# Graph-attention kernel on one core: segment maxima split into three bf16 terms and looked up in one bf16 product

## The reference

```
def seg_softmax(att, idx, n):
    m = jax.ops.segment_max(att, idx, num_segments=n)
    e = jnp.exp(att - m[idx])
    s = jax.ops.segment_sum(e, idx, num_segments=n)
    return e / (s[idx] + 1e-16)
...
att = seg_softmax(att, col, n)
att_i = seg_softmax(att_i, row, n)
res = (v * att[:, :, None]).reshape(-1, H * DK)
...
agg = jax.ops.segment_sum(res, col, num_segments=n) + jax.ops.segment_sum(res_i, row, num_segments=n)
```

## Time and profile before

| what | value |
|---|---|
| median of 3 runs | 4742.64 us (4734.96 to 4743.93) |
| span of the profiled execution | 4777.7 us |
| first sum stage, first to last `sums` product | about 3000.8 to 3318 us of the span |
| second sum stage, likewise | 4065.1 to 4385 us of the span |
| TensorE busy over the span | 2872.2 us (60%) |
| VectorE busy over the span | 2426.9 us (51%) |

### The profile page before, as it was taken

The page is one execution under the profiler, slowest core; times in us unless marked ns, Lnnn a source line. Parts: engine busy times, 40 slices in busy tenths (PEclk is TensorE's granted clock), DMA queues, the critical chain, the costliest instruction groups (busy, mean ns, idle before and its releaser), DMA issues.

```text
span 4777.7 us, 52094 instructions
## 1 busy us (share of the span) xinstructions
PE 2872.2 (60%) x13590; PEld 1938.9 (41%) x13692; DVE 2426.9 (51%) x4965; ACT 1720.4 (36%) x4345; POOL 2723.8 (57%) x2661
## 2 busy tenths in 40 slices
PE   3200025555533239367677777997777776997588
PEld 1000013333332126223444444887444444886445
DVE  7444444544421001433667677566677777566353
ACT  2232300000011002222455554786555554885451
POOL 5676756666645740466555554788555553555551
PEclk6555557767665569767777777999777777998799
DMA  4343356333414224267766667687777666665300
GB/s 143 113 172 126 143 111 231 89 89 91 98 57 165 97 89 148 68 200 212 216 199 208 200 200 184 177 213 184 205 202 209 201 202 166 160 173 149 110 1 27
DMA packets 767484, 720.00 MB, mean 151 GB/s; under 512 B 389089, under 2 KB 661163, under 8 KB 767068
## 3 DMA queue, kind: packets, MB, share of 16 engines
q1 hardware_dynamic: 645116, 399.08, 29.2%
q0 software_dynamic: 115136, 314.24, 22.4%
q10 hardware_dynamic: 6944, 3.34, 0.2%
HBM read 482.09 MB, written 243.22 MB: 152 GB/s over the span
## 4 chain that ended last, share of the span: by engine, by line
PE 22%; another core or an unknown queue 17%; DVE 16%; issue 12%; ACT 9%; DVEq 4%; POOL 2%; ACTq 2%; DMA 1%; SPq 1%; POOLq 0%
DVE META L1380 5%; DVE BIGR L605 3%; ACT AR L1674 3%; DVE AR L1400 3%; PE ps L1657 2%; PE ps L933 2%; PE ps L944 2%; ACT AR L1676 2%; DVE AR L596 2%; DVEq L1396 2%; PE ps L1480 1%; PE ps L1478 1%; ACTq L1675 1%; PE ps L1428 1%
## 5 line engine op out<-in xcount | busy, mean ns | idle before, releaser
L1349 POOL DMA_INDIRECT AR<-kv_tab,META x832 | 793.7, 954 | 620.8 <-DVE AR L1393 363.1
L1380 DVE TENSOR_REDUCE META<-ps 128x8 f32<-128x1024 f32 x416 | 508.5, 1223 | 186.3 <-remote 94.2
L493 POOL DMA_INDIRECT rec_dst<-AR,slot_e x400 | 403.3, 1008 | 229.1 <-issue 171.0
L625 PE MATMUL ps<-AR 128*128 128x256 f32 x832 | 318.2, 550 | 345.4 <-DVE AR L596 156.4
L579 POOL DMA_INDIRECT AR<-xn_tab,META x416 | 398.6, 958 | 206.8 <-issue 139.0
L1618 POOL TENSOR_TENSOR AR<-AR 128x896 f32<-128x896 f32 x208 | 351.4, 1689 | 246.1 <-ACT AR L1683 241.6
L1583 DVE TENSOR_TENSOR BIGR<-BIGR,ps 128x260 f32 x832 | 354.3, 426 | 217.4 <-PE ps L1657 131.1
L1478 PE MATMUL ps<-AR,identb 128*128 128x512 bf16 x832 | 403.8, 485 | 79.1 <-issue 55.2
L1657 PE MATMUL ps<-AR 128*128 128x260 f32 x1664 | 413.9, 392 | 2.1 <-POOL AR L1618 2.0
L625 PEld LDWEIGHTS ps<-AR 128*128 128x128 f32 x832 | 219.7, 277 | 445.1 <-issue 214.9
L1526 ACT ACTIVATE AR<-ps 12x512 bf16<-12x512 bf16 x208 | 122.1, 587 | 671.8 <-remote 469.9
(11 more groups left out here) (430 smaller groups left out, 5624.0 us busy)
## 6 DMA issues: line engine op xcount, KB each, us to landing
v_dst<-AR SPq DMA_DIRECT2D x104, 384.0 KB
AR<-v_dst SPq DMA_DIRECT2D x104, 384.0 KB
v_src<-AR SPq DMA_DIRECT2D x104, 384.0 KB
AR<-v_src SPq DMA_DIRECT2D x104, 384.0 KB
AR<-in_W_qvk SPq DMA_DIRECT2D x44, 608.0 KB
rec_raw<-AR SPq DMA_DIRECT2D x40, 640.0 KB
AR<-rec_dst SPq DMA_DIRECT2D x104, 192.0 KB
AR<-rec_src SPq DMA_DIRECT2D x104, 192.0 KB
```

Source lines behind the costliest of these rows:

```text
L493: pool.indirect_dma_start(rec_tab[0], bass.IndirectOffsetOnAxis(ap=slot_e[0][:, c * CC + k:c * CC + k + 1].bitcast(U32), axis=0), RD[s][0] ...
L625: ins = pe.matmul(l0_ps(s, u), OW[s][:, u, :], GA[s][:, u, :], start=True, stop=True)
L1349: pool.indirect_dma_start(KVR[s][:, u, 0:KV], None, kv_tab, bass.IndirectOffsetOnAxis(ap=META[o][:, g * U + u, 0:1].bitcast(U32), axis=0)) ...
L1380: ve.tensor_reduce(BMALL[o][:, g * U + 2 * half:g * U + 2 * half + 2, :].rearrange("p b h -> p (b h)"), PSA[:, 2048 + 1024 * half:3072 + 1 ...
```

## The change

The maxima are no longer kept in f32 for the product. After the scans, VectorE splits each f32 maximum into three bf16 terms `M3` (the upper half of the number, the upper half of the rest, and what remains). `lookup` then multiplies the transposed one-hot, now stored in bf16, with the 12 columns of three terms by four heads. `argument` first adds the three terms on VectorE into `MSUM` and then subtracts as before. Buffers move in SBUF to make room.

```
-        OH = [ar(7680 + 512 * s, U, P) for s in range(SL)]
-        OT = [ar(9728 + 512 * s, U, P) for s in range(2)]
+        OH = [ar(8641 + 512 * s, U, P) for s in range(SL)]
+        OT = [ar(a, U, P, dt=BF16) for a in (11201, 5504)]
+        MSUM = [ar(a, U * H1) for a in (7680, 7696)]
...
-        DIST2 = [DIST, ar(11330, U, P)]
+        DIST2 = [ar(a, U, P) for a in (10689, 4992)]
...
-        MT = ar(4160, NB, H1)
+        M3 = AR[:, 4160:4160 + 3 * 3649].bitcast(BF16).rearrange("p (k n) -> p k n", k=3)[:, :, 0:NB * H1].rearrange("p k (b h) -> p k b h", h=H1)
+        MT, MREST = ar(5760, NB, H1), ar(8641, NB, H1)
...
             for h in range(H1):
-                ins = ve.tensor_tensor_scan(MT[:, ::-1, h], EDGE[:, NB:0:-1], BMALL[o][:, ::-1, h], -1.0e30, ALU.add, ALU.max)
-            ins.then_inc(sem("pass_set"), 1)
+                ve.tensor_tensor_scan(MT[:, ::-1, h], EDGE[:, NB:0:-1], BMALL[o][:, ::-1, h], -1.0e30, ALU.add, ALU.max)
+            ve.drain()
+
+            def upper(x):
+                return x.rearrange("p b h -> p (b h)").bitcast(BF16).rearrange("p (b h two) -> p b h two", h=H1, two=2)[:, :, :, 1]
+
+            ve.tensor_copy(M3[:, 0, :, :], upper(MT))
+            ve.tensor_tensor(MREST, MT, upper(MT), ALU.subtract)
+            ve.drain()
+            ve.tensor_copy(M3[:, 1, :, :], upper(MREST))
+            ve.tensor_tensor(M3[:, 2, :, :], MREST, upper(MREST), ALU.subtract).then_inc(sem("pass_set"), 1)
             ve.drain()
...
+                ve.tensor_reduce(MSUM[g % 2], PS[2 + g % 2][:, 0:3 * NW].rearrange("p (u k h) -> p u h k", k=3, h=H1), AX.X, ALU.add)
+                ve.drain()
                 ve.tensor_tensor(ARG[g % 2], ATT[:, g * U:(g + 1) * U, :].rearrange("p u h -> p (u h)"),
-                                 PS[2 + g % 2][:, 0:U * H1], ALU.subtract).then_inc(sem("arg"), 1)
+                                 MSUM[g % 2], ALU.subtract).then_inc(sem("arg"), 1)
...
-                    ins = pe.matmul(PS[2 + g % 2][:, u * H1:(u + 1) * H1], OT[g % 2][:, u, :], MT[:, g * U + u, :],
+                    ins = pe.matmul(PS[2 + g % 2][:, 3 * u * H1:3 * (u + 1) * H1], OT[g % 2][:, u, :], M3[:, :, g * U + u, :],
                                     start=True, stop=True, skip_group_check=True)
```

## The result

| | before | after |
|---|---|---|
| median | 4741.52 us (4727.95 to 4765.68, 12 runs) | 4762.31 us (4756.35 to 4771.09, 12 runs) |
| ratio, 95% interval | | 1.005 (1.0039 to 1.0062) |
| span of the profiled execution | 4777.7 us | 4766.8 us |

The change makes the kernel slower. The medians lie 20.8 us apart, and the interval of the ratio stands for 18 to 29 us. The forecast was 4758 us, and the measured median is 4.3 us above it, inside the range. The two spans seem to say the opposite, because the score stages, which the change does not touch, took different times in the two profiled executions. So the two traces are compared stage by stage, never by their spans.

What follows compares the result with a forecast made beforehand. ScalarE's loop was taken to bound the sum stages at 3.05 us a step. Split +11.9, steady state +4.1, ramp -1.1 and tail +0.6 gave +15.5 us on 4742.64, so 4758 us, range 4746 to 4774.

Steps and rivals of the forecast that it cites:

- ScalarE's loop sets the step: Sum stages: copies through Relu, then the wait for transposes, give 3.05 us a step, which the change does not shorten.
- TensorE and ScalarE are nearly full, within 0.01 us of each other: Sum-stage step: TensorE's lookup ends at 4204.21, ScalarE's Relu at 4204.22, so both engines have almost no room.
- TensorE was the bound: Rival, chance 0.05: TensorE sets the sum-stage step, which falls to 2.93 us; kernel faster, 4730 us.
- The split, +11.9 us: Between scans and sum stage: four uncovered VectorE operations cost 5.96 us a pass, +11.9 us in two passes.
- The reduction takes 250 ns: VectorE, each sum-stage group: adding 48 elements takes 250 ns, with a 0.07 us drain delaying the subtraction 0.32 us.
- The steady state, +4 us: Sum stages: 0.32 us delay overdraws 0.29 us slack in a two-step loop through VectorE; +4 us, 0 to +7.
- The ramp, -1.1 us: Start of each sum stage, where TensorE is late: the shorter product saves 0.55 us, twice, -1.1 us.
- The tail, +0.6 us: Last step of each pass: the exponential waits for the subtraction, adding 0.32 us, twice, +0.6 us.
- Only the split costs: Rival, chance 0.18: reduction takes 206 ns and its delay fits the sum-stage slack; +11.4 down to +7, 4750 to 4754 us.
- VectorE costs more: Rival, chance 0.12: reduction and drain take 0.42 us in each sum-stage step; steady steps +13, total +25, 4767 us.
- The clock falls: Rival, chance 0.05: idling TensorE drops to half clock in a tenth of the sum-stage steps; +36 us, 4794 us.
- The new addresses: Rival, chance 0.03: OH and DIST2 start at odd words, costing 0.05 us a step, +10 us, 4768 us.

Runs made afterwards that it cites:

- e4_one_term: Kernel before with subtracted maxima and transposed one-hot in bf16, one bf16 product, no split or reduction: 3954.45 us, ratio 0.9987 to the kernel before.
- e5_before_fill: Kernel before with two of the next group's four Abs put ahead of the copies on ScalarE: 3930.25 against 3960.92 us, ratio 0.9915.
- e2_reduce_only: Kernel before with a 48-element reduction and a drain ahead of each subtraction, f32 product, no split: 3969.08 us, ratio 1.0025 to the kernel before.
- e3_add_in_psum: Kernel after with three bf16 products a block adding the terms in PSUM, no reduction or drain: 3970.85 us, ratio 1.0024 to the kernel before.
- e9_after_again: Kernel after, unchanged, on a chip of the experiments: 3977.84 against 3957.87 us for the kernel before, ratio 1.0049.

## Why the prediction was right, point by point

- *ScalarE's loop sets the step.* Right for the kernel before. The one-term kernel takes 23 us in 100 from TensorE and the step stays at 3.05 us, and filling ScalarE's pause shortens it to 2.84.
- *The 0.05 us between Relu and transposes is the passing of the signal.* Right, but the row that I gave for it doesn't bear it. I wrote that TensorE stood idle before its transposes at 2995.69. It did not: the lookup before them, in a stretch with the granted clock at 0.50 (1.2 GHz), ran to 2993.83 + 1.87 = 2995.70. The rows that show it are those of after and of the one-term kernel, where TensorE had waited 0.76 us and also started 0.05 us behind the Relu.
- *TensorE and ScalarE are nearly full, within 0.01 us of each other.* Wrong by 0.2 us. TensorE's own loop is 2.84 us. I had taken the end of the lookup, 4204.21, as the time at which TensorE could begin its transposes. But transposes may start 0.14 us before the last lookup ends. The trace before held this: behind the ramp, where TensorE was late, transposes start 0.81 us behind the lookup (4068.53 to the earlier trace rows's 4069.34), while in the steady state it is 1.01. The rows of before (timeline, TensorE) that say both are these:

```profile
2993.83 1.87 PE L1647 MATMUL ps<-AR 128*128 128x4 f32 x8 [0.69 <-ACT AR L1667]
...
4068.53 0.95 PE L1647 MATMUL ps<-AR 128*128 128x4 f32 x8
```

  It did not harm the forecast, since it only made TensorE's rival weaker, but it cost me the expectation of e5_before_fill by 22 us.
- *The split, +11.9 us.* Right: 12.0 in the trace, 12.5 alone. The copy keeps its 0.52 ns an element on every second half (1.03 us for 1664), and each copy even overlaps the next operation by 0.09 us. In the first pass 0.42 us passed before the first copy, where the drain's 0.07 was expected; those 0.35 us more are one of VectorE's pauses, at its place in the count of 128.
- *The reduction takes 250 ns.* Wrong, 208 ns: its elements alone (206). Groups of 3 cost nothing extra, and L1194, whose price for a group I took, reads groups of 4 from SBUF. The subtraction is later by 0.28 us and not 0.32, exactly the lower end of the prediction. By the prediction's own working that should have fitted the slack of 0.29, and the term been nothing.
- *The steady state, +4 us.* This is the term that was mis-sized. The stages grow by 7.9 us from first to last copies, and since the ramps give back 0.9 of that, the steady steps cost 8.8 us, above the end of +7. I computed one ordinary step. That step was nearly right (+0.01 us, 1.8 us in all). The other 7 us come from the steps in which VectorE pauses 0.35 us: some 12 in each pass, each now 0.27 us longer than before, make 2 x 12 x 0.27 = 6.5, and some 3 pauses more in all, which the added instructions bring, make about 1. The prediction had allowed for late fetches only within its upper end, and gave them no price. The slack of 0.27 us that the reduction used up was no idle reserve; it had been absorbing the pauses. Two errors of opposite sign, 250 ns for 208 and no pauses, met in a value that came near.
- *The ramp, -1.1 us.* The lookup is shorter by 0.70 and not 0.55 us, but the first full steps lasted 3.76 and 3.91 us in place of 4.11 and 4.42: -0.9 us.
- *The tail, +0.6 us.* Right. The last exponentials wait 2.84 us for the subtraction, where the earlier trace rows had 2.57: 0.27 us, twice.
- *The sum,* with the measured terms: 12.0 + 8.8 - 0.9 + 0.5 = 20.4 us, which is also what lies between the two ends in the trace, against 20.8 between the medians.

The rivals. *Only the split costs* fell with e2_reduce_only, where the reduction alone costs 10 us, although its premise (206 ns) was the true one. Had VectorE never paused, the terms left would be 12.0 + 1.8 - 0.9 + 0.5 = 13.4 us, near its 11.4; that is an estimate. *TensorE was the bound* fell with e4_one_term; so the rule of the Trainium skill (Perfetto Trace Analysis, Identifying the Most-Contended Engine), to judge TensorE's room by the busy share of its weight loads and to optimize the most contended engine first, does not hold for this case: weight loads went from 87 to 61 us in 100 for -0.13%. *VectorE costs more* was wrong in its mechanism, as each operation costs less than assumed, and its +13 us for the steady state misses the 8.8 by about as much on the high side as my +4.1 on the low side; it too put the loss in the two-step loop. *The clock falls* fell: 1.00 in the middle of the stage with TensorE at 74 us in 100. *The new addresses* fell with e3_add_in_psum. The rule of the Trainium skill (VectorE: DVE Perf Modes, TRN2 errata) gives 0.175 us for the reduction; measured are 0.208, and the rows' own line gave 206 ns.

What is shown and what is only argued: that the reduction costs 8 to 10 us and the split 12 is shown by the runs that have only one of them. That the pauses carry most of the reduction's cost is read from the traces (3.41 us for 3.14 in paused steps, 13 steps over 3.3 us for 3). That they follow the count of VectorE's instructions is read from the traces as well. No run took the pauses away or moved them, and what VectorE does in them stays open: the profile gives no releaser for them.

## What to carry to other kernels

Slack in a loop that seems unused may be absorbing irregular delays of an engine; before spending it, look at the distribution of the steps and not at one of them, and price a delay d against slack s and pauses p as max(0, p + d - s) less max(0, p - s) for each pause. Added instructions can also make the pauses more frequent. An engine's busy share says little about its room when its operations overlap: add the shortest start-to-start distances of its operations, taken where it is the late one (here 0.22 + 1.81 + 0.81 = 2.84 in a step of 3.05, at 97.55% busy). And when one engine waits a fixed time in each step for the answer of another, fill that wait with work that is ready: here that was worth 31 us, while making the other engine's lookup four times shorter was worth about 4 by the medians and 1.3 in the sum stages.

## What the runs showed of the hardware that was not expected

- VectorE pauses for about 0.35 us (0.55 in place of 0.20 before an `add`) with no wait behind it in the profile. In the sum stages of all twelve traces these pauses lie 128 of its recorded instructions apart, or a multiple of it: about 26.2 us in the kernel before with 15 instructions a step, 23.4 us in the kernel after with 17.
- In the ramps of the sum stages TensorE's granted clock rose from 0.50 to 1.00 at different times behind the first sums: 2.7 us in before's first pass, 3.4 us in after's, about 8 us in that of e2_reduce_only. There it cost 2.4 us.
- A reduction of 16 groups of 3 from PSUM takes 208 ns, no more than its 48 elements; these short groups cost nothing extra.
- The chips of the timing and of the experiments differ widely in the stages that move data, and hardly in the sum stages. The kernel after in its first score stage, on the chip of the timing (columns as in rows 1):

```profile
2250.00:2957.00 707.00, 524.39 (x2788) 318.42 (x2788) 500.23 (x747) 366.54 (x960) 397.20 (x417) 0.76 0.71 208
```

and the same kernel, e9_after_again, on a chip of the experiments, likewise in a score stage, and behind it its sum stage:

```profile
1700.00:2300.00 600.00, 467.02 (x2774) 278.50 (x2820) 498.16 (x774) 367.17 (x957) 448.12 (x469) 0.94 0.89 271
3300.00:3400.00 100.00, 73.52 (x515) 60.27 (x516) 67.14 (x194) 81.03 (x225) 54.37 (x33) 1.00 0.68 169
```

271 GB/s and a clock of 0.94 against 208 and 0.76; about the same TensorE instructions in 600 us as in 707. The sum stages show the same busy times in 100 us on both, within 1 us. Which part of the chip makes the difference was not tried. It is why all comparisons here are made against the kernel before on the same chip, and in microseconds and not in per cent where two kinds of chip are set side by side.
